# Attention and routing with a split mixture of experts: a tile's shift issued in its own step instead of the next one, in half of the steps

## The chip, the cores and the metric

The kernel runs on one core of one Trainium2 chip. The metric is the device time of one execution in microseconds (us), lower being better. The kernel before takes 2149.16 us as the median of 3 runs (2145.25 to 2153.57).

## The reference

The input `x` is 8192 tokens (4 sequences of 2048) of 512 features, float32. The output is a block in two halves, each of the form `x = x + layernorm(f(layernorm(x)))`:

```python
x = x + _layernorm(_L0_attn_ref(_layernorm(x), w_qkv, w_out, sorf_signs, sorf_scales))
x = x + _layernorm(_L0_ffn_ref(_layernorm(x), gate_w, bias, W1, W3, W2, sw1, sw3, sw2))
```

`_L0_attn_ref` is linear attention with 16 heads of 32: random features `q_phi` and `k_phi` (exponentials of a projection), a sum over the sequence `S = k_phi^T v` and `sum_k`, then per token `numer = q_phi S`, `denom = max(q_phi sum_k, 1e-6)`, `out = (numer / denom) @ w_out.T`. `_L0_ffn_ref` routes each token to 4 of 32 experts (sigmoid scores, top 4, a position within the expert's 512 places), runs a gated MLP for each expert and a shared one for all tokens, and sums them with the routing weights.

## The kernel before

The program has four stages, one after the other, each a block of five instruction streams (TensorE, ScalarE, VectorE, GpSimd, SyncE) that wait for each other by semaphores; a stage ends when all its streams have ended. They are: setup and projection to q, k, v; sums over the sequence; `attend_and_route_stage` (lines 758 to 1285), which the change touches; and experts with the combination at the end.

`attend_and_route_stage` goes over 16 groups of 512 tokens, each of 4 tiles of 128 tokens (64 tiles). Its order is written out by hand: every stream runs the same loop over steps `s`, and in step `s` it does for tile `s - lag` the part of the work that has this lag. The lags are constants (line 769): PROJECT 8, MEASURE 9, SCALE 10, ADD 11, SPLIT 12, TURN 13, GATE 14 and so on. Parts that are done once for each group of 4 tiles run where `group_at(s, lag)` gives a group, that is in every fourth step.

What each stream does in a step, as far as it matters here:

- TensorE (lines 950 to 967): feature logits and the products with the sums for unit `s` (lines 875, 885, 894), `project` of tile `s - 8` (12 matmuls, line 906), `turn` (918) and the gate product (932). `project` of tile `m` waits for `z_ready` of tile `m - 2`, since there are two PSUM tiles `y`. The product for `total` of a new group waits for `den_ready`.
- ScalarE (lines 1045 to 1072): two exponentials `phi` (976), `make_z` of tile `s - 10` (997), which waits for `shift_ready`, `read_numer` (984), `copy_turned` (1019), `normalize` of tile `s - 12` (1005 and 1011), and in every fourth step `make_at_high` (990).
- GpSimd (lines 1279 to 1283): `make_rstd` of unit `s - 9` in two instructions (1262 adds epsilon, 1264 takes the power -1/2), then `send` of tile `s - 21`: 4 indirect DMAs (1271) that write the routing records of the tile. The first tile of a group waits for `slots_ready`, which VectorE's `fill` gives.
- VectorE (lines 1214 to 1250): the list below.
- SyncE (line 838): for each group, when `den` is written by VectorE, it stores it in memory, loads it back spread over the partitions as `dens`, stores the reciprocals `share` and loads them back as `spread`.

VectorE's step, in its order: `read_total` (1099, every fourth step) writes `den`; `make_shift` (1125) computes `-mean * rstd` of unit `s - SCALE = s - 10`; `read_position` (1187); `make_low` (1156); `add` (1137); `measure_y` (1130); `measure_x1` (1141); `aggregate` of unit `s - 9` (1147 and 1150), which gives `mv_ready` to GpSimd; then the parts of a group. With `s mod 4` these are:

- 0: `read_total` at the step's start, `make_share` (reciprocals, 1106) at its end, which waits for the DMA of `dens`
- 1: `fill` (1192 to 1205), which ends with `slots_ready`
- 2: `divide` (the product with the reciprocals, 1111, 128 x 2048), which waits for the DMA of `spread`, and then `choose` (1161 to 1174, top 4 and one-hot)
- 3: `make_at_low` (the low halves, 1115, 128 x 2048), and then `weigh` (1178 to 1183)

A unit `u` carries two things in one set of statistics: those of the attention output of tile `u` (column 0) and those of the sum `x1` of tile `u - 2` (column 1). There are 66 units. `make_shift` of unit `u` waits for these (lines 1120 to 1124):

```python
dve.wait_ge(rstd_ready, u + 1)
if u >= 2:
    dve.wait_ge(z_ready, min(u - 1, NT))
if u >= 4:
    dve.wait_ge(xn_ready, u - 3)
```

Both streams run their instructions strictly in this order, so whatever stands behind a wait on VectorE waits too.

Of the kernel before, what the change touches and what calls it, by code (L numbers as in the profile page):

```python
# [15 lines left out]
A = G // P  # L16
# [741 lines left out]
def attend_and_route_stage(nc, io, keep):  # L758
# [5 lines left out]
    with ExitStack() as ctx:  # L764
# [4 lines left out]
        PROJECT, MEASURE, SCALE, ADD, SPLIT, TURN, COPY, GATE = 8, 9, 10, 11, 12, 13, 14, 14  # L769
# [46 lines left out]
        UNITS = NT + ADD - MEASURE  # L816
        STEPS = 4 * (NG - 1) + SEND + A
        block = ctx.enter_context(nc.Block())

        def group_at(s, lag):  # L820

            return (s - lag) // A if s >= lag and (s - lag) % A == 0 and (s - lag) // A < NG else None
# [257 lines left out]
        def _(dve):  # L1080
# [14 lines left out]
            def read_total(n):  # L1095
                dve.wait_ge(total_ready, EC * (n + 1))
                if n >= 1:
                    dve.wait_ge(den_stored, 16 * HPC * n)
                nc.vector.tensor_scalar(den[:], total[:], 1.0 / AT_SCALE, 1e-6 * M / AT_SCALE, ALU.mult,
                                        ALU.max).then_inc(den_ready, 1)  # L1100

            def make_share(n):
                dve.wait_ge(dens_loaded, 16 * (n + 1))
                if n >= 1:
                    dve.wait_ge(share_stored, 16 * n)
                nc.vector.reciprocal(share[:], dens[:]).then_inc(share_ready, 1)

            def divide(n):
                dve.wait_ge(spread_loaded, 16 * HPC * (n + 1))
                dve.wait_ge(numer_read, EC * (n + 1))  # L1110
                nc.vector.tensor_tensor(heads[n % 2][:], heads[n % 2][:], spread[:], ALU.mult).then_inc(at_ready, 1)

            def make_at_low(n):
                dve.wait_ge(at_high_ready, n + 1)
                nc.vector.tensor_tensor(at_hl[n % 2][:, 1], heads[n % 2][:], at_hl[n % 2][:, 0],
                                        ALU.subtract).then_inc(at_low_ready, 1)

            def make_shift(u):
                k = u % 2
# [5 lines that stand above are left out]
                nc.vector.scalar_tensor_tensor(out=shift[k][:], in0=mv[k][:, :, 0], scalar=-1.0, in1=rstd[k][:],  # L1125
                                               op0=ALU.mult, op1=ALU.mult).then_inc(shift_ready, 1)

            def measure_y(m):
                dve.wait_ge(y_ready, m + 1)
                nc.vector.bn_stats(stats[m % 2][:, 0, :], y[m % 2][:]).then_inc(y_measured, 1)  # L1130

            def add(m):
                n, a = m // A, m % A
                dve.wait_ge(z_ready, m + 1)
                if a == 0:
                    dve.wait_ge(x_loaded[n % XS], 16 * (n // XS) + 16)
                nc.vector.tensor_tensor(x[n % XS][:, a, :], x[n % XS][:, a, :], z[m % 2][:], ALU.add).then_inc(x1_ready, 1)

            def measure_x1(m):
                dve.wait_ge(x1_ready, m + 1)  # L1140
                nc.vector.bn_stats(stats[m % 2][:, 1, :], x[m // A % XS][:, m % A, :]).then_inc(x1_measured, 1)

            def aggregate(u):
                k = u % 2
                if u < NT:
                    dve.wait_ge(y_measured, u + 1)
                    ins = nc.vector.bn_aggr(mv[k][:, 0, :], stats[k][:, 0, :])
                if u >= ADD - MEASURE:
                    dve.wait_ge(x1_measured, u - (ADD - MEASURE) + 1)
                    ins = nc.vector.bn_aggr(mv[k][:, 1, :], stats[k][:, 1, :])  # L1150
                ins.then_inc(mv_ready, 1)

            def make_low(m):
                n, a = m // A, m % A
                dve.wait_ge(x_high_ready, m + 1)
                nc.vector.tensor_tensor(hl[n % 2][:, a, 1, :], xn[m % 2][:], hl[n % 2][:, a, 0, :],
                                        ALU.subtract).then_inc(x_low_ready, 1)

            def choose(n):
                dve.wait_ge(score_ready, n + 1)  # L1160
                then(nc.vector.tensor_scalar(score[:], grown[:], 1.0, None, ALU.add))
                then(nc.vector.reciprocal(score[:], score[:]))
                then(nc.vector.tensor_tensor(biased[:], score[:], bias, ALU.add))
                for a in range(A):
                    ins = nc.vector.max(top[:, a, :], biased[:, a, :])
                then(ins)
                for a in range(A):
                    ins = nc.vector.max_index(index[:, a, :], top[:, a, :], biased[:, a, :])
                then(ins)
                then(nc.vector.tensor_copy(chosen[:], index[:, :, 0:K]))  # L1170
                then(nc.vector.tensor_tensor(onehot[:], number, chosen[:].unsqueeze(3).broadcast_to([P, A, K, NE]),
                                             ALU.is_equal))
                with nc.allow_low_precision(reason="sums of zeros and one 1"):
                    ins = nc.vector.tensor_reduce(mask[:], onehot[:].rearrange("p a j e -> p a e j"), AX.X, ALU.add)
                ins.then_inc(mask_ready, 1)

            def weigh(n):
                then(nc.vector.tensor_tensor(picked[:], onehot[:], per_choice(score[:]), ALU.mult))
                then(nc.vector.tensor_reduce(w[:], picked[:], AX.X, ALU.add))
                then(nc.vector.tensor_reduce(weight_sum[:], w[:], AX.X, ALU.add))  # L1180
                then(nc.vector.tensor_scalar(weight_sum[:], weight_sum[:], 1e-12, None, ALU.max))
                then(nc.vector.reciprocal(weight_sum[:], weight_sum[:]))
                then(nc.vector.tensor_tensor(w[:], w[:], weight_sum[:].unsqueeze(2).broadcast_to([P, A, K]), ALU.mult))

            def read_position(n):
                dve.wait_ge(position_ready, n + 1)
                nc.vector.tensor_copy(where[:].rearrange("p a e -> p (a e)"), position).then_inc(where_ready, 1)
# [26 lines left out]
            for s in range(STEPS):  # L1214
                n = group_at(s, A)
                if n is not None:
                    read_total(n)
                if 0 <= s - SCALE < UNITS:
                    make_shift(s - SCALE)
                n = group_at(s, PLACE + 1)  # L1220
                if n is not None:
                    read_position(n)
                if 0 <= s - TURN < NT:
                    make_low(s - TURN)
                if 0 <= s - ADD < NT:
                    add(s - ADD)
                if 0 <= s - MEASURE < NT:
                    measure_y(s - MEASURE)
                if 0 <= s - ADD < NT:
                    measure_x1(s - ADD)  # L1230
                if 0 <= s - MEASURE < UNITS:
                    aggregate(s - MEASURE)
                n = group_at(s, A)
                if n is not None:
                    make_share(n)
                n = group_at(s, A + 2)
                if n is not None:
                    divide(n)
                n = group_at(s, A + 3)
                if n is not None:  # L1240
                    make_at_low(n)
                n = group_at(s, CHOOSE)
                if n is not None:
                    choose(n)
                n = group_at(s, WEIGH)
                if n is not None:
                    weigh(n)
                n = group_at(s, FILL)
                if n is not None:
                    fill(n)  # L1250
# [517 lines left out]
```

## Time and profile before

| | |
|---|---|
| median of 3 runs | 2149.16 us (2145.25 to 2153.57) |
| profiled execution | 2154.41 us |
| its span, first to last instruction | 2152.6 us |
| mean granted TensorE clock in it | 0.944 |
| TensorE matmul busy | 1828.6 us (85%) |
| VectorE busy | 1205.9 us (56%) |
| ScalarE busy | 1124.9 us (52%) |
| GpSimd busy | 772.0 us (36%) |

PE is the matmul part of TensorE and PEld its weight loads, DVE is VectorE, ACT ScalarE, POOL GpSimd, SPq the queue of SyncE. In all rows times are in us unless marked ns, and `L1125` is line 1125 of the kernel. A row of a timeline has the start, the duration, the engine, the line, the operation, output and inputs, shapes and, in brackets, how long the engine had been idle before and what released it. A row of waits has who waited, for whom, the total, how many times and the longest. The stage `attend_and_route_stage` runs from about 870 to 1465 us of the span; its first steps have no choosing and no sends yet, its last steps have no logits any more.

### The profile page before, as it was taken

Reading aid. Unit: us, or ns where it says so; the run is one execution under the profiler, and the core shown is the slowest. Engines: PE = TensorE matmul, PEld = TensorE weight load, DVE = VectorE, ACT = ScalarE, POOL = GpSimd, SP = SyncE. Lnnn points to the kernel's source line nnn. Section 1 sums busy time; section 2 is a strip of 40 time slices with the busy share of each in tenths; the row PEclk is TensorE's granted clock in tenths of the full one; section 3 lists DMA queues with packets and bytes.
Section 4 is the critical chain, followed back from the end, with each engine's and each line's share of the span. In section 5 each row is a group of like instructions: output and inputs, shape, how many; then the busy total and the mean of one; then the engine's idle time right before and its main releaser. Section 6 shows DMA issues by size and latency. Waiting matters only on the chain. (4 is left out here: it accounts for less than half of the span.)

```text
span 2152.6 us, 33711 instructions
## 1 busy us (share of the span) xinstructions
PE 1828.6 (85%) x12976; PEld 890.7 (41%) x12976; DVE 1205.9 (56%) x2230; ACT 1124.9 (52%) x1371; POOL 772.0 (36%) x718
## 2 busy tenths in 40 slices
PE   8899999999979999799888898404999988987995
PEld 6444444444427877133333333202444444433342
DVE  7676667666650000158878888831444434435887
ACT  5564555545425665577777776402444444432443
POOL 0000000000000000025677788874777777751110
PEclk9999999999989999899999999756999999998998
DMA  7435353546238886578777875322789999876994
GB/s 257 144 123 187 108 200 106 163 148 211 90 113 220 212 211 160 131 182 238 217 213 221 249 219 169 137 72 90 168 194 267 250 257 227 176 138 169 352 343 155
DMA packets 187791, 403.05 MB, mean 187 GB/s; under 512 B 33780, under 2 KB 72052, under 8 KB 171008
## 3 DMA queue, kind: packets, MB, share of 16 engines
q1 hardware_dynamic: 83184, 222.41, 35.2%
q10 hardware_dynamic: 67584, 122.17, 16.3%
q0 software_dynamic: 36864, 56.32, 13.7%
q8 instruction: 103, 1.69, 0.3%
q14 instruction: 56, 0.46, 0.1%
HBM read 237.06 MB, written 174.98 MB: 191 GB/s over the span
## 5 line engine op out<-in xcount | busy, mean ns | idle before, releaser
L258 PE MATMUL s_proj<-s_xT,keep_wqkv 128*128 128x512 f16 x1536 | 341.8, 379 | 0.0
L1271 POOL DMA_INDIRECT slot_dram<-s_filled,s_slots x256 | 305.2, 1192 | 95.1 <-issue 72.9
L1415 POOL DMA_INDIRECT acc_dram<-s_y,s_slot x128 | 205.9, 1609 | 101.3 <-DMA acc_dram<-s_y,s_slot 47.1
L906 PE MATMUL s_y<-keep_wo,s_at_hl 128*128 128x512 f16 x768 | 194.7, 408 | 42.6 <-ACT s_z L997 42.6
L258 PEld LDWEIGHTS s_proj<-s_xT,keep_wqkv 128*128 128x128 f16 x1536 | 147.8, 98 | 183.2 <-issue 12.6
L237 PE MATMUL s_proj<-keep_wqkv,s_xT 128*128 128x512 f16 x768 | 179.7, 393 | 34.5 <-ACT s_xT L500 34.5
L1522 ACT ACTIVATE s_gate<-s_gates 128x512 f32<-128x512 f32 x96 | 57.3, 597 | 281.2 <-PE s_ups L1474 219.1
L339 POOL TENSOR_SCALAR s_rstd<-s_mv 128x4 f32<-128x4 f32 x16 | 16.0, 998 | 496.5 <-DVE s_mv L354 496.5
L518 ACT ACTIVATE s_hl<-s_rot 128x1024 f16<-128x1024 f32 x64 | 67.6, 1057 | 221.1 <-DVE s_rot L400 220.6
L1577 DVE SCALAR_TENSOR_TENSOR s_h<-s_gate,s_ups 128x512 f32<-128x512 f32 x96 | 65.9, 686 | 199.0 <-ACT s_gate L1522 199.0
L676 ACT ACTIVATE s_phi<-s_logits 128x1024 f32<-128x1024 f32 x128 | 131.1, 1024 | 84.5 <-PE s_logits L697 84.5
L387 DVE TENSOR_TENSOR s_by_cos<-s_proj,s_table 128x1024 f32<-128x1024 f32 x64 | 78.4, 1224 | 171.4 <-PE s_proj L258 171.4
L1513 ACT ACTIVATE s_xT<-s_turned 128x1024 f16<-128x1024 f16 x128 | 125.5, 1019 | 83.3 <-PE s_turned L1452 83.0
L976 ACT ACTIVATE s_phi<-s_logits 128x1024 f32<-128x1024 f32 x128 | 131.1, 1024 | 53.4 <-PE s_logits L875 52.7
L1452 PE MATMUL s_turned<-keep_ident,s_rows 128*128 128x128 f16 x1024 | 80.3, 223 | 84.5 <-DMA s_rows<-rows_dram,s_slot 76.2
L1404 POOL DMA_INDIRECT s_rows<-rows_dram,s_slot x128 | 132.2, 1033 | 47.1 <-issue 36.9
L906 PEld LDWEIGHTS s_y<-keep_wo,s_at_hl 128*128 128x128 f16 x768 | 74.0, 103 | 179.2 <-issue 57.0
L737 PE MATMUL s_parts<-s_phi,s_v 128*33 128x128 f32 x2048 | 138.6, 278 | 2.2 <-DMA s_v<-v_dram 2.1
L1474 PE MATMUL s_gates<-s_xT,s_w 128*128 128x512 f16 x512 | 124.4, 387 | 18.6 <-issue 9.7
L1488 PE MATMUL s_ys<-s_w,s_parts 128*128 128x512 bf16 x512 | 132.1, 382 | 3.5 <-DVE s_y L1592 3.5
L237 PEld LDWEIGHTS s_proj<-keep_wqkv,s_xT 128*128 128x128 f16 x768 | 75.3, 101 | 132.0 <-ACT s_xT L500 42.2
L1474 PE MATMUL s_ups<-s_xT,s_w 128*128 128x512 f16 x512 | 121.3, 380 | 0.0
(164 smaller groups left out, 3217.0 us busy)
## 6 DMA issues: line engine op xcount, KB each, us to landing
s_x<-x_in SPq DMA_DIRECT2D x32, 1024.0 KB, 9.8
qk_dram<-s_hl ACTq DMA_DIRECT2D x32, 1024.0 KB
keep_ahead<-qk_dram SPq DMA_DIRECT2D x48, 512.0 KB
acc_dram<-s_zero SPq DMA_DIRECT2D x17, 1024.0 KB, 11.5
v_dram<-s_v ACTq DMA_DIRECT2D x16, 1056.0 KB, 5.8
s_v<-v_dram SPq DMA_DIRECT2D x16, 1056.0 KB
s_spread<-share_dram SPq DMA_DIRECT2D x64, 256.0 KB, 4.6
x_dram<-s_x ACTq DMA_DIRECT2D x16, 1024.0 KB, 4.9
```

The source lines that it names most:

```text
L237: mm = nc.tensor.matmul(proj[half][:, 512 * b:512 * b + 512], left, right, start=(c == 0 and i == 0), stop=(c == EC - 1 and i == 2))
L258: mm = nc.tensor.matmul(out[:, 512 * b:512 * b + 512], left, right, start=(c == 0 and i == 0), stop=(c == EC - 1 and i == 2))
L676: nc.scalar.activation(phi[n % 2][:].rearrange("p h m -> p (h m)"), logits[n % 2][:], ACT.Exp, scale=1.0 / M_SCALE).then_inc(phi_ready, 1)
L737: mm = nc.tensor.matmul(parts[ch % 2][at:at + D + 1, h // 2 * M:(h // 2 + 1) * M], v[n % 2][:, a * H + h, :], phi[half][:, h % HALF, :], s ...
L906: mm = nc.tensor.matmul(y[m % 2][:], at_hl[n % 2][:, s, c, a * P:(a + 1) * P], keep["wo"][:, w, c, :], start=(c == 0 and i == 0), stop=(c ...
L976: nc.scalar.activation(phi[m % PHIS][:].rearrange("p h q -> p (h q)"), logits[:], ACT.Exp, scale=1.0 / M_SCALE).then_inc(phi_ready, 1)
L1271: nc.gpsimd.indirect_dma_start(out=io["slot"], out_offset=bass.IndirectOffsetOnAxis(ap=slots[n % 2][:, a * K + j:a * K + j + 1], axis=0), ...
L1404: nc.gpsimd.indirect_dma_start(out=rows[r][:, a, :], out_offset=None, in_=io["rows"], in_offset=bass.IndirectOffsetOnAxis(ap=slot[e % RING ...
L1415: nc.gpsimd.indirect_dma_start(out=io["acc"], out_offset=bass.IndirectOffsetOnAxis(ap=slot[e % RING][:, a, 0:1], axis=0), in_=y[e % 2][:, ...
L1474: mm = nc.tensor.matmul(bank[:], w[:, c, i * P:(i + 1) * P], left[:, s, c, :], start=(c == 0 and s == 0), stop=(c == EC - 1 and s == 1))
L1488: mm = nc.tensor.matmul(ys[a % 2][:], parts[e % 2][:, i, s, a * P:(a + 1) * P], w[:, i, :], start=(i == 0 and s == 0), stop=(i == IC - 1 a ...
L1513: nc.scalar.activation(xT[k][:, :, :, a * P:(a + 1) * P], turned[a % 2][:].bitcast(F16).rearrange("p (s c q) -> p s c q", s=2, c=EC), ACT. ...
```

## The change

In the steps in which `divide` or `make_at_low` runs (`s mod 4` of 2 and 3, from step 6 on), `make_shift` of the unit that this step has aggregated is issued in the same step, behind `divide` or `make_at_low` and ahead of `choose` or `weigh`. It is left out at the start of the step after. In the other steps nothing changes. The units moved are 1 and 2, 5 and 6, up to 57 and 58: 30 of 66. No instruction is added or removed.

```diff
+        def shifted_early(s):
+
+            return group_at(s, A + 2) is not None or group_at(s, A + 3) is not None
+
@@
                 n = group_at(s, A)
                 if n is not None:
                     read_total(n)
-                if 0 <= s - SCALE < UNITS:
+                if 0 <= s - SCALE < UNITS and not shifted_early(s - 1):
                     make_shift(s - SCALE)
@@
                 n = group_at(s, A + 3)
                 if n is not None:
                     make_at_low(n)
+                if 0 <= s - MEASURE < UNITS and shifted_early(s):
+                    make_shift(s - MEASURE)
                 n = group_at(s, CHOOSE)
                 if n is not None:
                     choose(n)
```

## Rows read from the trace of the kernel before

**Rows 1.** The page: busy time of each engine, share of the span, instructions.
```profile
PE 1828.6 (85%) x12976; PEld 890.7 (41%) x12976; DVE 1205.9 (56%) x2230; ACT 1124.9 (52%) x1371; POOL 772.0 (36%) x718
```

**Rows 2.** Busy time by stretch of the span: length, engines, clock, DMA share, GB/s.
```profile
914.00:978.00 64.00, 60.13 (x407) 20.70 (x400) 39.88 (x84) 48.96 (x61) 14.36 (x19) 1.00 0.78 199
978.00:1340.00 362.00, 310.80 (x2370) 117.67 (x2369) 304.21 (x776) 267.79 (x342) 270.17 (x270) 0.95 0.73 214
```

**Rows 3.** Everything that DVE waited for from 978 to 1340 us.
```profile
DVE s_share L1106 <- DMA s_dens<-den_dram: 33.4, 12, 8.3
DVE s_shift L1125 <- POOL s_rstd L1264: 9.8, 10, 3.4
DVE s_heads L1111 <- DMA s_spread<-share_dram: 6.5, 5, 3.9
```

**Rows 4.** The wait for z on PE, for the shift on ACT, 978 to 1340.
```profile
PE s_y L906 <- ACT s_z L997: 24.5, 14, 5.0
...
ACT s_z L997 <- DVE s_shift L1125: 51.0, 25, 5.8
```

**Rows 5.** Timeline of DVE in steps 46 and 47: divide, choose, shift, low halves, shift.
```profile
1191.18 2.27 DVE L1111 TENSOR_TENSOR s_heads<-s_heads,s_spread 128x2048 f32<-128x2048 f32 x1
...
1198.16 0.15 DVE L1125 SCALAR_TENSOR_TENSOR s_shift<-s_mv,s_rstd 128x2 f32<-128x2 f32 x1
...
1200.85 2.26 DVE L1115 TENSOR_TENSOR s_at_hl<-s_heads,s_at_hl 128x2048 f16<-128x2048 f32 x1
...
1205.90 0.15 DVE L1125 SCALAR_TENSOR_TENSOR s_shift<-s_mv,s_rstd 128x2 f32<-128x2 f32 x1
```

**Rows 6.** Timeline of POOL in the same two steps.
```profile
1189.37 1.39 POOL L1271 DMA_INDIRECT slot_dram<-s_filled,s_slots  x1 [2.28 <-DVE s_slots L1205]
...
1195.59 0.22 POOL L1262 TENSOR_TENSOR s_rstd<-s_mv,s_eps 128x2 f32<-128x2 f32 x1
1195.89 0.72 POOL L1264 TENSOR_TENSOR s_rstd<-s_rstd,s_power 128x2 f32<-128x2 f32 x1
...
1204.26 0.72 POOL L1264 TENSOR_TENSOR s_rstd<-s_rstd,s_power 128x2 f32<-128x2 f32 x1
```

**Rows 7.** ACT's xn of tile 33, which the shift of unit 37 needs.
```profile
1185.75 0.83 ACT L1005 ACTIVATE s_xn<-s_x,s_shift,s_rstd 128x512 f32<-128x512 f32 x1
```

**Rows 8.** Divide (DVE) of steps 22, 38 and 66; the late shift behind step 50.
```profile
999.77 2.29 DVE L1111 TENSOR_TENSOR s_heads<-s_heads,s_spread 128x2048 f32<-128x2048 f32 x1 [0.43 <-DMA s_spread<-share_dram]
...
1130.73 2.29 DVE L1111 TENSOR_TENSOR s_heads<-s_heads,s_spread 128x2048 f32<-128x2048 f32 x1 [3.88 <-DMA s_spread<-share_dram]
...
1231.21 0.16 DVE L1125 SCALAR_TENSOR_TENSOR s_shift<-s_mv,s_rstd 128x2 f32<-128x2 f32 x1 [3.38 <-POOL s_rstd L1264]
...
1344.10 2.29 DVE L1111 TENSOR_TENSOR s_heads<-s_heads,s_spread 128x2048 f32<-128x2048 f32 x1 [0.85 <-DMA s_spread<-share_dram]
```

**Rows 9.** The powers (POOL) that belong to steps 22 and 66.
```profile
1004.49 0.72 POOL L1264 TENSOR_TENSOR s_rstd<-s_rstd,s_power 128x2 f32<-128x2 f32 x1
...
1348.81 0.72 POOL L1264 TENSOR_TENSOR s_rstd<-s_rstd,s_power 128x2 f32<-128x2 f32 x1
```

**Rows 10.** POOL in step 11, where it is idle when the statistics come.
```profile
925.56 2.15 POOL L1262 TENSOR_TENSOR s_rstd<-s_mv,s_eps 128x2 f32<-128x2 f32 x1 [6.18 <-DVE s_mv L1150]
927.79 0.69 POOL L1264 TENSOR_TENSOR s_rstd<-s_rstd,s_power 128x2 f32<-128x2 f32 x1
```

**Rows 11.** DVE in step 11: the low halves.
```profile
925.40 2.27 DVE L1115 TENSOR_TENSOR s_at_hl<-s_heads,s_at_hl 128x2048 f16<-128x2048 f32 x1
```

**Rows 12.** Waits of the queue of SP, 900 to 1420 us.
```profile
SPq L843 <- DVE s_den L1099: 213.3, 15, 20.7
```

**Rows 13.** Shift of unit 59 (DVE), at the start of step 69.
```profile
1364.26 0.16 DVE L1125 SCALAR_TENSOR_TENSOR s_shift<-s_mv,s_rstd 128x2 f32<-128x2 f32 x1 [3.03 <-POOL s_rstd L1264]
```

**Rows 14.** DVE's last instruction of the stage, and POOL's last.
```profile
1421.90 0.19 DVE L1205 CAST s_slots<-s_place 128x16 uint32<-128x16 f32 x1
...
1460.17 0.97 POOL L1271 DMA_INDIRECT slot_dram<-s_filled,s_slots  x1 [0.30 <-issue]
```

## The prediction

> **What bounds the kernel now.** The page names TensorE as the busiest engine by far [rows 1], so the first question is whether the stage that the change touches follows that average. A table by stretches answers it. From 914 to 978 us TensorE is busy 60.1 of 64 us and VectorE 39.9; from 978 to 1340 us, where every group of 4 steps also chooses, weighs and sends, TensorE is busy 310.8 of 362 us, VectorE 304.2 and GpSimd 270.2 [rows 2]. No engine fills that stretch, so a cycle of waits has to. I look at who waits for whom, VectorE first. Its whole idle time there is 49.7 us: 33.4 for the DMA of `dens`, 9.8 for GpSimd's `rstd`, 6.5 for the DMA of `spread` [rows 3]. What matters is what is missing: VectorE never waits for TensorE or ScalarE. They wait for it: ScalarE 51.0 us for the shift, TensorE 24.5 us for `z` behind that [rows 4]. The two DMAs on which VectorE waits start from VectorE's own writes, `den` and `share`; the SyncE queue had waited 213.3 us for `den` [rows 12]. So the cycle that sets the stage's pace from step 18 to 66 is VectorE's instruction order, its two round trips through memory, and GpSimd where VectorE waits for it. A microsecond of new waiting on VectorE is a microsecond of stage; a microsecond given to ScalarE or TensorE is worth nothing until they bind.
>
> **What the moved instruction finds.** The shift itself costs 0.15 us wherever it stands [rows 5]; no work is added, no DMA is moved, and SyncE's order stays. What moves is a blocking wait for `rstd`. Take unit 37. The product with the reciprocals starts at 1191.18 and takes 2.27, so it ends at 1193.45; then comes `choose`, and the shift at 1198.16 finds `rstd` ready [rows 5]. `rstd` ended at 1195.89 + 0.72 = 1196.61, since GpSimd was still busy with the four sends that began at 1189.37, when `fill` had given the slots, and took `rstd` only behind them [rows 6]. Issued behind the product, the shift blocks VectorE for 1196.61 - 1193.45 = 3.16 us, with `choose` queued behind it. `choose` and all that follows start that much later; before, `choose` covered this wait. The sends that delay `rstd` start from VectorE's own slots, so they don't come earlier relative to it and the wait repeats in each group. The other two conditions of the shift are no problem: the `xn` that it needs was written from 1185.75 on, ten microseconds earlier [rows 7].
>
> **The divide steps.** I subtract the end of the product from the end of `rstd` for each. In step 22 that is (1004.49 + 0.72) - (999.77 + 2.29) = 3.15 us, in step 66 (1348.81 + 0.72) - (1344.10 + 2.29) = 3.14 [rows 8, 9]; nine of the twelve steps from 22 to 66 lie between 3.14 and 3.16. The others: step 38 gives nothing, since the product itself came 3.88 us late from its DMA [rows 8]; step 34 gives 1.9, for the same reason; step 50 gives 8.1, of which VectorE already waited 3.38 later, at the shift [rows 8], so 4.7 is new. Step 18, with no sends ahead of it, gives 0.8. The sum is 9 x 3.15 + 1.9 + 4.7 + 0.8 = 35.8 us.
>
> **The steps with low halves.** In step 47 the low halves end at 1200.85 + 2.26 = 1203.11 [rows 5] and `rstd` at 1204.26 + 0.72 = 1204.98 [rows 6]: 1.87 us by the same subtraction. But GpSimd was late there only because it was still behind from the step before. After the change VectorE has just waited 3.15 us, GpSimd has caught up and is idle when the statistics arrive. The nearest row for that is step 11: there GpSimd's first instruction starts with the low halves, takes 2.15 us instead of 0.22 [rows 6, 10], and the power ends at 927.79 + 0.69 = 928.48, 0.81 after the low halves (925.40 + 2.27) [rows 10, 11]. I take 0.82 for the 13 steps from 19 to 67, 10.7 us, with 0 and 1.87 as ends.
>
> The row shows that the small instruction does not pass beside the product. The Trainium skill, page "SBUF — State Buffer", section "Who interferes with whom", has a rule that speaks against this change here: a VectorE instruction with two SBUF inputs and a GpSimd instruction that reads SBUF exclude each other, and whichever starts second waits for all of the first. By that rule, the trace agrees (2.15 against 0.22 us); if it did not hold here, `rstd` would be ready inside the low halves, those steps would cost nothing, and the sum would be 10.7 us smaller.
>
> **What is given back.** With VectorE some 4 us later in each group, GpSimd is no longer late at the ordinary shifts of the steps `s mod 4` of 0 and 1: of the 9.8 us [rows 3], 3.4 are counted above, and the other 6.4 go. At the end GpSimd binds: the shift of unit 59 waited 3.03 us for it [rows 13], and GpSimd's sends run on to 1461 while VectorE ended at 1422 [rows 14]. So of the last pair of stalls, 3.14 + 0.82 = 3.96 us in steps 66 and 67, only what delays GpSimd counts: it takes up `rstd` of unit 58 at the end of the later low halves, so that `rstd` ends 3.14 + 0.82 - 1.87 = 2.1 us later than before. 1.9 us go. The earlier shifts also free ScalarE and TensorE (`z` of unit 37 some 1.5 us earlier); I cost that at nothing, since VectorE waits for neither. Steps 10 to 15 cost nothing either: there the shift was waited for anyway or TensorE binds [rows 2].
>
> **The sum.** 35.8 + 10.7 - 6.4 - 1.9 = 38.2 us. The profiled execution took 2154.4 us, 5.2 above the median of 2149.16 (0.24%, less than the 0.5% that a measurement of this kernel can tell from no change). On the profiled time that makes 2192.6, on the median 2187.4. I give 2187.
>
> **The rivals.**
>
> *It is slower by more.* If GpSimd does not catch up, each low-halves step costs its 1.87 and nothing is given back: 35.8 + 13 x 1.87 = 60 us, 2209. For it: the 1.87 stands in nine of the thirteen steps. Against it: GpSimd idled 2.28 us per group waiting for slots [rows 6], so it has the room. Chance 0.1.
>
> *The wait is swallowed.* VectorE waits 33.4 us for `dens` anyway, 2.8 a group [rows 3]. If that DMA landed when the traffic lets it, not a fixed time after `den`, a later `den` would wait less, and 38 - 33 = 5 us would be left: 2154, no change that can be measured. For it: these waits vary up to 8.3 us. Against it: SyncE stood ready and waiting for `den` each time [rows 12], so the transfer starts later by all of the delay. Chance 0.07.
>
> *It is faster.* If the stage follows TensorE, the 24.5 us that it waits for `z` [rows 4] shrink, since `z` follows the earlier shift at once: 2149 - 24 = 2125. The mechanism is project, `y`, `measure_y`: it decides from the point where VectorE waits for `y` in the steps 22 to 66. For it: TensorE is the busiest engine there by 6.6 us [rows 2]. Against it: VectorE did not wait for `y` once [rows 3]. Chance 0.05. The Trainium skill, page "Perfetto Trace Analysis", section "Identifying the Most-Contended Engine", says to take the engine with the highest occupancy as the bottleneck and to work on its gaps, with a caution about matmul time; by that rule the time would be this rival's, and the trace disagrees with it here.
>
> *Part of the price is paid elsewhere.* If half of the stall is hidden by shorter DMA waits, because the longer groups leave less traffic at a time, 38.2 - 0.5 x 33.4 = 21.5 us remain: 2171. That lies inside my range; chance 0.13. That the change does nothing at all can be left out: the wait stands where it is written, and VectorE runs in order.
>
> **How the numbers follow.** The forecast, about 38 us with the low-halves steps between 0 and their upper end, has 0.65; with the two cases on its own side (0.1 and 0.13) slower has 0.88, same 0.07, faster 0.05. The range runs from 2165, a little below the half-hidden case, to 2209, the case without catching up. It leaves out the swallowed and the faster case, 0.12 together, and some chance above.
>
> **What the new profile would show.** VectorE's wait for `rstd` at line 1125 should rise from 9.8 to about 50 us in the stretch from step 18 to 67, in two sizes, near 3.15 us behind line 1111 and near 0.8 us behind line 1115; GpSimd's wait for slots grows from 2.3 to some 6 us a group; the `dens` wait stays near 2.8 us a group; a group, from product to product, takes 34 to 35 us where it took (1344.10 - 999.77) / 11 = 31.3 [rows 8]. The other stages keep their lengths. I am wrong if the stall at line 1111 is much shorter (the sends then moved too), if the `dens` waits shrink with it, or if VectorE's busy neighbours, not its waits, turn out to set the group's length.

## The result and the profile after

The changed kernel takes 2186.72 us (median of 4 runs, 2185.37 to 2188.0), the kernel before 2147.2 (median of 4, 2143.3 to 2153.57): 1.0169 times as long, 95% interval 1.0139 to 1.0200, which is some 36 us (the two medians lie 39.5 us apart). The forecast was 2187 with a range of 2165 to 2209.

The page of the changed kernel, span and busy time of each engine:

```profile
span 2185.5 us, 33665 instructions
...
PE 1838.8 (84%) x12930; PEld 891.7 (41%) x12976; DVE 1207.7 (55%) x2230; ACT 1122.9 (51%) x1371; POOL 777.2 (36%) x718
```

VectorE is as busy as before, to 2 us [rows 1], over a span 33 us longer: the time is waiting. The spans differ by less than the medians because the profiled execution of before, 2154.41 us, was longer than all four of its timed ones. To find the waiting I cut the same piece of work out of both traces, from the product of step 18 to the shift of unit 59. The kernel before needs 393 us for it, the changed one 424; 31 of the 33 us are there. Busy time by stretch, first before, then after (length, VectorE busy, TensorE's clock, DMA share, GB/s):

```profile
971.28:1364.30 393.02, 330.63 (x847) 0.95 0.73 214
```

```profile
973.90:1397.80 423.90, 332.84 (x847) 0.91 0.69 199
```

What VectorE waited for in that piece, in the kernel before:

```profile
DVE s_share L1106 <- DMA s_dens<-den_dram: 33.4, 12, 8.3
DVE s_shift L1125 <- POOL s_rstd L1264: 12.9, 11, 3.4
DVE s_heads L1111 <- DMA s_spread<-share_dram: 7.3, 6, 3.9
```

and in the changed kernel:

```profile
DVE s_shift L1129 <- POOL s_rstd L1270: 42.1, 27, 4.5
DVE s_share L1110 <- DMA s_dens<-den_dram: 21.6, 12, 4.3
DVE s_hl L1160 <- ACT s_hl L1015: 12.5, 9, 1.7
DVE s_heads L1115 <- DMA s_spread<-share_dram: 3.9, 3, 1.8
DVE s_stats L1134 <- PE s_y L910: 2.1, 4, 0.6
```

So the wait for `rstd` at the shift rose by 29.2; the `dens` wait fell by 11.8 and the `spread` wait by 3.4; two waits are new, 12.5 for ScalarE at `make_low` and 2.1 for TensorE at `measure_y`; busy time grew by 2.2. The sum, 29.2 - 11.8 - 3.4 + 12.5 + 2.1 + 2.2, is 30.8 of the 30.9 us. That it closes says where the time is and not yet why: the waits and the work of any engine add up to the length.

One group of the changed kernel, VectorE's waits from step 45 to 47 with the product and the low halves (a timeline; the brackets give the idle time and what ended it):

```profile
1197.47 0.56 DVE L1110 RECIPROCAL s_share<-s_dens 128x64 f32<-128x64 f32 x1 [1.38 <-DMA s_dens<-den_dram]
...
1205.52 0.69 DVE L1160 TENSOR_TENSOR s_hl<-s_xn,s_hl 128x512 f16<-128x512 f32 x1 [1.58 <-ACT s_hl L1015]
...
1208.15 2.27 DVE L1115 TENSOR_TENSOR s_heads<-s_heads,s_spread 128x2048 f32<-128x2048 f32 x1
...
1212.33 0.16 DVE L1129 SCALAR_TENSOR_TENSOR s_shift<-s_mv,s_rstd 128x2 f32<-128x2 f32 x1 [1.90 <-POOL s_rstd L1270]
...
1219.78 2.26 DVE L1119 TENSOR_TENSOR s_at_hl<-s_heads,s_at_hl 128x2048 f16<-128x2048 f32 x1
...
1222.92 0.16 DVE L1129 SCALAR_TENSOR_TENSOR s_shift<-s_mv,s_rstd 128x2 f32<-128x2 f32 x1 [0.89 <-POOL s_rstd L1270]
```

GpSimd in the same group:

```profile
1208.64 2.62 POOL L1277 DMA_INDIRECT slot_dram<-s_filled,s_slots  x1 [0.30 <-issue]
1211.28 0.22 POOL L1268 TENSOR_TENSOR s_rstd<-s_mv,s_eps 128x2 f32<-128x2 f32 x1
...
1219.95 2.14 POOL L1268 TENSOR_TENSOR s_rstd<-s_mv,s_eps 128x2 f32<-128x2 f32 x1 [2.58 <-DVE s_mv L1154]
1222.17 0.72 POOL L1270 TENSOR_TENSOR s_rstd<-s_rstd,s_power 128x2 f32<-128x2 f32 x1
```

The blocked shift is there in both steps, 1.90 us behind the product and 0.89 behind the low halves; both answer to places where [rows 5] has no wait at all. Behind the low halves GpSimd had been idle for 2.58 us, so it had caught up as forecast. Behind the product the wait is shorter than the 3.16 us that rows 5 and 6 gave. VectorE reaches the product later, here by the new wait at 1205.52, while GpSimd goes on sending, so the send that the product holds up (2.62 us) is the last of the four. In the kernel before it was the third, and one more of 0.97 + 0.30 us followed it: 3.16 - 1.27 is 1.89. From the end of `fill` to the product it takes 3.8 to 4.5 us in the ten steps with the short wait, and 2.6 to 3.5 in the nine steps of the kernel before that gave 3.15. In steps 26 and 66 the DMA of `spread` makes it longer, in step 42 that DMA and ScalarE, in the other seven ScalarE alone.

Where the wait for ScalarE comes from is seen on TensorE. Its waits in the same piece, before and then in the changed kernel:

```profile
PE s_y L906 <- ACT s_z L997: 35.1, 17, 7.0
...
PE s_total L894 <- DVE s_den L1099: 5.9, 7, 0.9
```

```profile
PE s_total L898 <- DVE s_den L1103: 45.2, 11, 4.8
PE s_y L910 <- ACT s_z L1001: 19.3, 6, 5.0
```

The earlier shift did what it was for: TensorE waits 19.3 us for `z` where it waited 35.1. But `den` comes late for it, and TensorE now stands 45.2 us (4.1 a group) before it may write the next total. Its logits come late, ScalarE's `phi` with them, and `make_low` waits for the tile behind that. Two things beside the stalls come in here. One is the earlier shift itself, which brings TensorE sooner to the place where it needs `den` (measured below, 22.8 us without any new stall). The other may be TensorE's clock. The rows show its eight matmuls for `total` behind such a wait, the same ones a step later, and the stretch of the first (length, busy times, and then the granted clock, the DMA share and GB/s):

```profile
1193.34 1.93 PE L898 MATMUL s_total<-s_phi,keep_sumk 128*32 128x512 f32 x8 [4.77 <-DVE s_den L1103]
...
1201.73 1.06 PE L898 MATMUL s_total<-s_phi,keep_sumk 128*32 128x512 f32 x8
```

```profile
1193.30:1195.30 2.00, 1.97 (x9) 0.30 (x10) 2.00 (x5) 1.56 (x3) 1.50 (x2) 0.50 0.09 25
```

After 4.77 us without work the granted clock was 0.50 (1.2 GHz, the lower of its two levels), and the same matmuls took 1.93 us instead of 1.06. Over the piece it fell from 0.95 to 0.91, and the matmuls' busy time rose from 329.8 to 341.6 us. No run separates what the clock adds to the 12.5 us at `make_low`.

### The profile page after: what moved, and what is told of

Same layout as the page of the kernel before. It is cut to its first block and busy times, and to the rows that moved or that the text cites. A ratio compares the mean times of both kernels' runs of the same rounds, so it can differ in the third digit from the quotient of the medians.

```text
span 2185.5 us, 33665 instructions
## 1 busy us (share of the span) xinstructions
PE 1838.8 (84%) x12930; PEld 891.7 (41%) x12976; DVE 1207.7 (55%) x2230; ACT 1122.9 (51%) x1371; POOL 777.2 (36%) x718
## 3 DMA queue, kind: packets, MB, share of 16 engines
q0 software_dynamic: 36864, 56.32, 13.3%
q8 instruction: 103, 1.69, 0.3%
## 5 line engine op out<-in xcount | busy, mean ns | idle before, releaser
L1277 POOL DMA_INDIRECT slot_dram<-s_filled,s_slots x256 | 288.9, 1129 | 92.7 <-issue 73.7
L1494 PE MATMUL s_ys<-s_w,s_parts 128*128 128x512 bf16 x480 | 126.2, 384 | 5.3 <-DVE s_y L1598 3.5
## 6 DMA issues: line engine op xcount, KB each, us to landing
s_v<-v_dram SPq DMA_DIRECT2D x16, 1056.0 KB, 10.9
```

The costliest lines, as they stand in the source:

```text
L1277: nc.gpsimd.indirect_dma_start(out=io["slot"], out_offset=bass.IndirectOffsetOnAxis(ap=slots[n % 2][:, a * K + j:a * K + j + 1], axis=0), ...
L1494: mm = nc.tensor.matmul(ys[a % 2][:], parts[e % 2][:, i, s, a * P:(a + 1) * P], w[:, i, :], start=(i == 0 and s == 0), stop=(i == IC - 1 a ...
```

## The experiments

All ratios are to the kernel before, timed in the same rounds; the changed kernel's is 1.0169 (1.0139 to 1.0200).

### One part at a time

Only the product steps:

```diff
-            return group_at(s, A + 2) is not None or group_at(s, A + 3) is not None
+            return group_at(s, A + 2) is not None
```

> Only the shifts of the steps with the product with the reciprocals are moved. If the cost is VectorE blocked on GpSimd's rstd behind each product, this part alone carries most of it: 35.8 us of waits as counted in the kernel before, less the 6.4 us of late-GpSimd waits that vanish, so about 29 us over the kernel before, near 2176. If instead the price came mainly from TensorE and ScalarE being starved by the later den, or if the two parts only hurt together, this kernel lies within 10 us of the kernel before.

Only the low-halves steps:

```diff
-            return group_at(s, A + 2) is not None or group_at(s, A + 3) is not None
+            return group_at(s, A + 3) is not None
```

> Only the shifts of the steps with the low halves are moved. By the theory, GpSimd has not been given time to catch up here, so the wait behind the low halves is the 1.87 us of the kernel before, not the 0.85 us seen with both parts: 13 x 1.87 = 24 us, less some of the 6.4 us that vanish, so 18 to 24 us over the kernel before, 2165 to 2171, and 2165 to 2171 plus e1 minus the kernel before is more than the whole change. If the wait there is a fixed 0.85 us, it costs about 11 us, 2158.

Measured: 2172.4 us, 1.0116 (1.0077 to 1.0155), and 2163.1 us, 1.0077 (1.0054 to 1.0099). Against 2149.8 for the kernel before, timed beside them, the parts cost 22.7 and 13.3 us, together 36.0. By the ratios they are 1.16% and 0.77%, together 1.93% against 1.69% for the whole change; the intervals cover the difference, so the parts add up. VectorE's waits with the product steps alone, from 975 to 1375:

```profile
DVE s_shift L1129 <- POOL s_rstd L1270: 34.7, 12, 4.8
DVE s_share L1110 <- DMA s_dens<-den_dram: 26.2, 12, 4.7
DVE s_hl L1160 <- ACT s_hl L1015: 6.0, 8, 1.6
```

and with the low-halves steps alone:

```profile
DVE s_share L1110 <- DMA s_dens<-den_dram: 29.4, 12, 9.7
DVE s_shift L1129 <- POOL s_rstd L1270: 16.6, 13, 1.9
DVE s_hl L1160 <- ACT s_hl L1015: 8.7, 8, 1.7
```

The first case gives 34.7 us of waits in the steps 22 to 66, where the forecast's own counts give 9 x 3.15 + 1.9 + 8.1 = 38.4 (its 35.8 leaves out the 3.4 that VectorE waited for step 50 already). It was expected at 29 us over the kernel before and came at 22.7, with the wait for `dens` down from 33.4 to 26.2. One by one, the waits come in sizes: 1.90 five times, 3.19 five times and twice more than 4.4. The second case missed my expectation of 18 to 24 us. Its 13 waits are 0.9 us eight times and 1.9 five times, not 1.87 throughout: where VectorE had waited for ScalarE a step earlier or the DMA was late, GpSimd had caught up there as well. Two waits of the kernel with the product steps alone:

```profile
1041.08 0.16 DVE L1129 SCALAR_TENSOR_TENSOR s_shift<-s_mv,s_rstd 128x2 f32<-128x2 f32 x1 [1.90 <-POOL s_rstd L1270]
...
1074.38 0.16 DVE L1129 SCALAR_TENSOR_TENSOR s_shift<-s_mv,s_rstd 128x2 f32<-128x2 f32 x1 [3.19 <-POOL s_rstd L1270]
```

1.90 to 3.19 is one send of GpSimd, 0.97 us and the 0.30 after it.

### The same shifts where `rstd` is ready

```diff
-            def choose(n):
+            def choose(n, shift=None):
...
                 then(nc.vector.tensor_copy(chosen[:], index[:, :, 0:K]))
+                if shift is not None:
+                    make_shift(shift)
...
-                if 0 <= s - MEASURE < UNITS and shifted_early(s):
-                    make_shift(s - MEASURE)
...
-                    choose(n)
+                    choose(n, s - MEASURE if shifted_early(s) and s - MEASURE < UNITS else None)
+                elif s >= MEASURE and group_at(s, A + 2) is not None:
+                    make_shift(s - MEASURE)
...
                     weigh(n)
+                if s >= MEASURE and group_at(s, A + 3) is not None:
+                    make_shift(s - MEASURE)
```

> The same 30 shifts leave the next step, but stand where rstd is ready by the trace of the kernel before: inside choose, behind the copy of the chosen indices, and at the end of weigh. If only the blocked wait costs and an earlier z is worth nothing, this runs as the kernel before within 0.3%, 2143 to 2153, with VectorE's wait for rstd at the shift not above 15 us in the stage. If an earlier z is worth time, because TensorE's wait of 24.5 us for z binds, it is 8 us or more faster than the kernel before.

Measured: 2152.3 us, 1.0015 (0.9993 to 1.0038). The 30 shifts have left the next step, `z` comes earlier, and neither a cost nor a gain can be measured. VectorE's wait for `rstd` from 975 to 1375, and TensorE's waits in the piece from the product of step 18 to the shift of unit 59:

```profile
DVE s_shift L1129 <- POOL s_rstd L1274: 10.1, 12, 3.0
```

```profile
PE s_y L910 <- ACT s_z L1001: 24.3, 8, 6.8
PE s_total L898 <- DVE s_den L1103: 22.8, 11, 2.7
```

The wait for `rstd` is no larger than the kernel before's 12.9 us in its piece. TensorE waits 10.8 us less for `z` and 16.9 more for `den`: the time that the earlier `z` gives it is spent at the next wait for VectorE. What costs is the wait ahead of `choose` and `weigh`, and the rival by which an earlier `z` is worth time has fallen.

### VectorE computes `rstd` itself

```diff
             def make_shift(u):
                 k = u % 2
-                dve.wait_ge(rstd_ready, u + 1)
+                dve.wait_ge(mv_ready, u + 1)
                 if u >= 2:
+                    dve.wait_ge(shift_ready, u - 1)
                     dve.wait_ge(z_ready, min(u - 1, NT))
...
+                nc.vector.tensor_tensor(rstd[k][:], mv[k][:, :, 1], eps[:], ALU.add).then_inc(var_ready, 1)
+                dve.wait_ge(var_ready, u + 1)
+                nc.vector.tensor_tensor(rstd[k][:], rstd[k][:], power[:], ALU.mult).then_inc(rstd_ready, 1)
+                dve.wait_ge(rstd_ready, u + 1)
...
-                if 0 <= s - MEASURE < UNITS:
-                    make_rstd(s - MEASURE)
```

(`power` is set to 1e-13 for the first column and 1 for the second. Both kernels leave out the power -1/2, so their output is not the reference's.) With the moved shift:

> The changed kernel, with VectorE computing rstd itself at the shift, in two small instructions, and GpSimd not at all. The power -1/2 is left out: the second instruction multiplies instead, so the scales of the normalizations are not those of the reference. By the theory the move costs only because the shift waits for GpSimd, so this kernel and its partner with the old place of the shift take the same time within 0.3% (6 us); both some 5 to 15 us over the kernel before, since VectorE has about 0.4 us more work a step and loses the 10 to 13 us of waits for rstd. If the place itself costs (through TensorE, ScalarE or a later den), this one is 15 us or more slower than its partner.

With the shift in its old place:

> The partner: the kernel before, with the same replacement of rstd (the power -1/2 left out, VectorE computes it). 2155 to 2165, and within 6 us of the partner with the moved shift. If an earlier z is worth time where nothing waits for GpSimd, the partner with the moved shift is faster than this one by more than 6 us.

Measured: 2158.2 us, 1.0026 (0.9998 to 1.0053), and 2152.3 us, 1.0001 (0.9978 to 1.0023). The two differ by 5.9 us, and their intervals overlap. In the profiles the piece from the product of step 18 to the shift of unit 59 takes 398 us with the moved shift and 399 with the old place. With GpSimd out of the way no cost of the move can be measured; the intervals leave room for up to some 13 us. TensorE's waits from 972 to 1396 us, moved first:

```profile
PE s_y L910 <- ACT s_z L1001: 29.3, 9, 5.6
PE s_total L898 <- DVE s_den L1103: 24.9, 11, 3.1
```

```profile
PE s_y L906 <- ACT s_z L997: 55.2, 32, 8.8
...
PE s_total L894 <- DVE s_den L1099: 9.4, 10, 0.9
```

Here too TensorE waits far less for `z` with the moved shift, and gains nothing by it; part of it comes back as waiting for `den`. The partner was expected at 2155 to 2165 and came at 2152: more than I had allowed for offset the extra work on VectorE. What did was not tried.

### One send fewer ahead of the product's `rstd`

```diff
-                for j in range(K):
+                turns = [(a, j) for j in range(K)]
+                if a == 0:
+                    turns = turns[:K - 1]
+                if a == 1:
+                    turns = [(0, K - 1)] + turns
+                for a, j in turns:
```

> The changed kernel, with GpSimd issuing the fourth send of a group's first tile behind the next rstd and not ahead of it. If the wait behind the product is GpSimd being late by its sends, it falls from 1.9 us to the 0.85 us that stand behind the low halves, 12 groups by 1.05 us: about 13 us faster than the changed kernel, 2174. If that wait has another source (the xn or z conditions of the shift), nothing changes: 2184 to 2190.

Measured: 2169.9 us, 1.0088 (1.0059 to 1.0118), some 17 us less than the changed kernel, where 13 were expected. One group of it, GpSimd first, then VectorE:

```profile
1201.02 2.13 POOL L1268 TENSOR_TENSOR s_rstd<-s_mv,s_eps 128x2 f32<-128x2 f32 x1
1203.23 0.72 POOL L1270 TENSOR_TENSOR s_rstd<-s_rstd,s_power 128x2 f32<-128x2 f32 x1
```

```profile
1200.82 2.27 DVE L1115 TENSOR_TENSOR s_heads<-s_heads,s_spread 128x2048 f32<-128x2048 f32 x1
...
1203.99 0.16 DVE L1129 SCALAR_TENSOR_TENSOR s_shift<-s_mv,s_rstd 128x2 f32<-128x2 f32 x1 [0.89 <-ACT s_xn L1009]
```

Three sends done, GpSimd takes `rstd` at once, is held by the product now, and the wait is 0.89 us instead of 1.90. The trace puts it down to `xn`, but `rstd` ended at 1203.23 + 0.72 = 1203.95, 0.04 us ahead of the shift: the last condition was `rstd` there as well. The wait is 0.89 us in seven of the twelve steps from 22 to 66 and longer in the others, where GpSimd was in a send when the product came. The waits behind the products sum to 19.8 us against 28.9 in the changed kernel, and the piece takes 413.0 us against 423.9.

### The shift ahead of the low halves

```diff
                 n = group_at(s, A + 3)
+                if 0 <= s - MEASURE < UNITS and n is not None:
+                    make_shift(s - MEASURE)
                 if n is not None:
                     make_at_low(n)
-                if 0 <= s - MEASURE < UNITS and shifted_early(s):
+                if 0 <= s - MEASURE < UNITS and group_at(s, A + 2) is not None:
                     make_shift(s - MEASURE)
```

> The changed kernel, with the shift of the low-halves steps issued ahead of the low halves and not behind them. If GpSimd's first rstd instruction takes 2.15 us there because the low halves hold it up, it now takes about 0.22 us, rstd is ready 1.05 us after the statistics, and VectorE waits some 1.1 us where it waited 0.85 behind the low halves: 13 x 0.25 = 3 us over the changed kernel, the same within the noise. If 2.15 us is simply what GpSimd needs from an idle start, the instruction keeps that length and VectorE waits 3 us in each such step: some 28 us over the changed kernel.

Measured: 2191.1 us, 1.0186 (1.0146 to 1.0226), the changed kernel's ratio within its interval. GpSimd and VectorE in a low-halves step:

```profile
1217.95 0.19 POOL L1270 TENSOR_TENSOR s_rstd<-s_mv,s_eps 128x2 f32<-128x2 f32 x1 [2.60 <-DVE s_mv L1154]
1218.21 0.72 POOL L1272 TENSOR_TENSOR s_rstd<-s_rstd,s_power 128x2 f32<-128x2 f32 x1
```

```profile
1218.97 0.16 DVE L1129 SCALAR_TENSOR_TENSOR s_shift<-s_mv,s_rstd 128x2 f32<-128x2 f32 x1 [1.11 <-POOL s_rstd L1272]
1219.05 2.28 DVE L1119 TENSOR_TENSOR s_at_hl<-s_heads,s_at_hl 128x2048 f16<-128x2048 f32 x1
```

The same instruction, from the same idle start, takes 0.19 us where it took 2.14 beside the low halves. The 2.14 is exclusion by the large product, as the rule of the Trainium skill (page "SBUF — State Buffer", section "Who interferes with whom") has it, and not what GpSimd needs to start.

### `den` written earlier

In the kernel before, and then in the changed kernel:

```diff
-                n = group_at(s, A)
-                if n is not None:
-                    read_total(n)
...
                 if 0 <= s - MEASURE < UNITS:
                     aggregate(s - MEASURE)
+                n = group_at(s, A - 1)
+                if n is not None:
+                    read_total(n)
```

> The kernel before with one other edit: VectorE reads the total into den in the step with the low halves, ahead of them, and not at the start of the next step. This starts the round trip through memory some 4.4 us earlier in each group. If VectorE's chain with its round trips and GpSimd behind it set the pace, the 33.4 us of waits for dens go and the kernel is 15 to 28 us faster, 2119 to 2132, with GpSimd (2.3 us of room a group) binding next. If the pace is TensorE's, or set by traffic, it is within 5 us of the kernel before.

> The changed kernel with den read ahead of the low halves. TensorE's wait for den and VectorE's new wait for ScalarE at make_low come, by the theory, from the later den, so both go, and the wait for dens too; in return GpSimd is given less time and the wait behind the product rises from 1.9 back to about 3.1 us. Net per group about 1.5 (dens) + 1.3 (make_low) - 1.2 = 1.6 us, 12 groups: 20 us faster than the changed kernel, 2167, still 15 to 25 us slower than the kernel with the early den and the shift in its old place. If the make_low wait comes from something else, it stays and the gain is under 10 us.

Measured: 2143.3 us, 0.9961 (0.9939 to 0.9983), faster than both kernels, but by 6 us on the medians and 8 by the ratio, where I expected 15 to 28; and 2166.9 us, 1.0077 (1.0047 to 1.0107), as expected. VectorE's waits in the first, 971 to 1364:

```profile
DVE s_shift L1125 <- POOL s_rstd L1264: 23.8, 20, 3.4
DVE s_share L1106 <- DMA s_dens<-den_dram: 20.3, 9, 8.7
```

The `dens` wait falls by 13.1 us, the wait for GpSimd rises by 10.9. GpSimd had less room than the 2.3 us a group that I gave it: it binds at once. In the second, 973 to 1396:

```profile
DVE s_shift L1129 <- POOL s_rstd L1270: 61.4, 34, 7.7
DVE s_share L1110 <- DMA s_dens<-den_dram: 8.6, 3, 5.7
```

No wait for ScalarE at `make_low` is left and none of TensorE for `den`, which shows that both came from `den` being late for TensorE; the granted clock in the piece is 0.96. The wait behind the product is back at its old size in ten of the twelve steps, since VectorE is no longer held that long ahead of it:

```profile
1171.32 0.16 DVE L1129 SCALAR_TENSOR_TENSOR s_shift<-s_mv,s_rstd 128x2 f32<-128x2 f32 x1 [3.17 <-POOL s_rstd L1270]
```

Behind the low halves there is no wait any more in 12 of the 13 steps: with the 0.69 us of `den` ahead of them, GpSimd's first instruction runs before they start, in 0.19 us.

The early den with the shifts placed where `rstd` is ready:

> The early den of the earlier run together with the shifts placed where rstd is ready. If GpSimd is the next bound, the shifts' place gives nothing and this takes the time of the early den alone, 2138 to 2150, within 5 us of it. If TensorE's 55 us of waits for z in that kernel bind, this is 8 us or more faster than it, under 2137. With GpSimd later in its group than before, a small new wait for rstd is possible and would make it slower by up to 10 us.

Measured: 2144.9 us, 0.9966 (0.9943 to 0.9988): the time of the early den alone, as expected. With VectorE waiting for GpSimd, an earlier shift gives nothing.

## Why the prediction was right

**The bound.** That VectorE's order, its round trips and GpSimd set the pace held: with the shifts' waits the kernel is slower, with the same shifts and no such waits it isn't, and TensorE's shorter wait for `z` bought nothing in the two kernels that have it without the stalls (the shifts where `rstd` is ready, and VectorE's own `rstd`). It was not the whole of it: 14.6 us of VectorE's new waits are for ScalarE and TensorE. The early `den` also shows how close GpSimd is behind the round trip of `dens`: 13.1 us of waits for one became 10.9 us of waits for the other.

**The divide steps** were 3.15 us each and 35.8 in all. By the same subtraction they measure 1.87 in ten of the steps, 4.44 in steps 22 and 50, and 0.82 in step 18. VectorE's waits there sum to 28.9 us, of which 3.4 (step 50) were there before, so 25.5 are new. Step 38, put at nothing because of its late DMA, cost 1.9 like the others. The step that failed is "the sends that delay `rstd` start from VectorE's own slots, so they don't come earlier relative to it": they do, as soon as something holds VectorE between the slots and the product. The new wait at `make_low` does, and in two of the ten steps the DMA of `spread`.

**The steps with low halves** were 0.82 us each; measured are 0.83 to 0.85, 13 times, as the row of step 11 had it [rows 10, 11]. That they would cost 1.87 without the product's stall ahead was wrong in most groups (eight of thirteen waits of 0.9), but the forecast did not rest on it.

**What is given back.** The ordinary shifts' waits for GpSimd, 6.4 us, are gone between steps 18 and 67. I said that the `dens` wait would stay, since the transfer starts later by all of the delay; it fell from 33.4 to 21.6. The transfer did start later, but it took less time: from the end of `den` to the reciprocals 5.7 us in the mean of these twelve groups before (4.1 to 11.1), 4.6 after (4.1 to 7.1), with the same 2.8 to 2.9 us of work between them. And "I cost that at nothing, since VectorE waits for neither" missed the other direction: TensorE comes sooner to where it needs `den`, `den` comes later, and VectorE then waits 12.5 + 2.1 us for ScalarE and TensorE.

**The hit and the luck.** In the piece the shifts' waits grew by 29.2 us where 38.2 was forecast, nearly all of the difference at the products. Against this stand -11.8 for `dens`, -3.4 for `spread`, +14.6 for ScalarE and TensorE and +2.2 of work, which nearly cancel. On the profiled times 2192.6 was forecast and 2187.3 measured, 32.9 us of cost and not 38.2. That the median fell on the forecast to 1 us is luck: the four runs of the kernel before have a median 2 us below the one that I added to. The mechanism, its place and its sign are shown; the waits at the shift were forecast at about 50 us and measured at 42.1.

**The signs named.** A group, from product to product, takes (1376.00 - 1004.59) / 11 = 33.8 us where 34 to 35 was forecast. Two signs of being wrong that I had named came in part: the stall behind the product is shorter, and the `dens` waits shrank. GpSimd's new idle time is not where I put it: its wait for slots stayed at 18.1 us in the piece (16.7 before), and its wait for the statistics rose from 27.2 to 55.5.

**The rivals.** Faster: fallen, by the kernel with the shifts where `rstd` is ready. The page of the Trainium skill that the prediction names beside it ("Perfetto Trace Analysis") doesn't speak for this rival as I had it: for TensorE its section goes by the rate of useful arithmetic and the weight loads' busy share in place of the matmuls' busy share, and the weight loads were busy for 117.67 of 362 us [rows 2]. Swallowed: a third of the wait for `dens` went, not all. Paid elsewhere in part: that third, where the rival had half. Slower by more: GpSimd did catch up. Why the `dens` round trip got shorter was not tried; the DMA share in the piece fell from 0.73 to 0.69, which would fit with less traffic in its way but does not show it.

## What to carry to other kernels

An instruction that only waits and does little may stand on an in-order engine only where its input is already there; find that place by subtracting, from the trace, the end of its input from the end of the work ahead of it. Work that stands ahead of such a wait is its cover, so moving the wait forward pays off only if the engine that is to be released sets the pace, and here it did not. When an engine is held, ask also who needs its next result: the stall came back through `den`, TensorE and ScalarE as a wait in another place.

## What the runs showed of the hardware

The wait behind a product comes in few sizes: mostly 0.89, 1.90 and 3.18 us, depending on whether GpSimd's `rstd` itself, its last send or the send before the last is caught by the product, and 4.47 where three sends still follow the product's start. GpSimd's small add takes 0.19 to 0.23 us beside nothing and 2.14 beside a 128 x 2048 instruction of VectorE with two inputs that started just before it. An indirect send takes 0.97 to 1.1 us in more than half of the cases and 1.4 to 1.6 in most of the others. In the kernel before and in the changed one, all 33 sends that start while such an instruction runs end 0.84 to 0.91 us behind it (2.62 us for the one shown, up to 3.07); a send that is under way when it starts isn't held (0.97 to 0.99 us, 29 times). TensorE's granted clock was 0.50 behind an idle time of 4.77 us and 1.00 from 1197.5 to 1199.3 us, some four microseconds later. Some sends come after an idle time that nothing in the profile explains, up to 6.6 us in the kernel before and 3.6 in the changed one.
